# A two-layer attention and mixture-of-experts kernel: the shared expert in one sequence with the destination table in parts, and the returned rows added ahead of the last results

## The chip, the cores and the metric

The kernel runs on one core of a Trainium2 chip. A core has five engines with instruction streams of their own: TensorE (PE, with its weight loads as PEld), VectorE (DVE), ScalarE (ACT), GpSimd (POOL) and SyncE (SP, which here issues transfers); 16 DMA engines carry the transfers of all of them. The metric is the device time of one execution in microseconds (us), the median of three runs.

## What is computed

`x` holds 16 sequences of 112 tokens, 256 wide, all in fp32. Cut to what matters:

```python
# layer zero: cross attention to ctx (16, 375, 256), then 8 experts, best one of 8, F = 704
x = x + tanh(g_xattn[0]) * xattn0(layernorm(x), ctx, mask)
x = x + tanh(g_ffn[0])   * ffn0(layernorm(x))
# layer one: another cross attention, then 8 experts, best two of 8, F = 512
x = x + tanh(g_xattn[1]) * xattn1(layernorm(x), ctx)
x = x + tanh(g_ffn[1])   * ffn1(layernorm(x))

def ffn0(x):                       # ffn1 alike, with two experts a token and softmax weights
    scores = x @ router            # (tokens, 8)
    gate = sigmoid(best score), else 0
    routed = sum over e of (silu(gate_e * x @ w1[e]) * (gate_e * x @ w3[e])) @ w2[e]
    shared = (silu(x @ ws1) * (x @ ws3)) @ ws2
    return shared + routed
```

Each token passes through the shared expert and through one (layer zero) or two (layer one) of eight routed experts.

## The kernel before

Each layer is a chain of stages: setup, attention, shared expert, routed experts. Each engine has a program of its own, written out by hand; semaphores join them, and an engine carries out its instructions in the order in which they are written.

**Attention** is a software-pipelined loop over the sequences; `body(i)` does a different step for several sequences at a time. In its last iterations `first_chunk(l, i - 15)` already makes the first products of the shared expert for the first group.

**Shared expert.** The 16 sequences are taken in groups of four (GT = 4, 448 columns). Of one group, the hidden width F is taken in chunks of 128 rows: six in layer zero (the last one half as high, with gate and up in one matmul, `both`, L1067), four in layer one. A chunk is two matmuls for gate and two for up (`group`, L1138); ACT makes the silu, POOL or DVE the product (POOL at L1782), and `back(g, c)` (L1108) is four matmuls, one for each sequence, that add the chunk's share of the result into PSUM banks 4 to 7. In the order below a matmul call stands once; fp32 calls show as two instructions in the trace, so a chunk has 8 instructions and a back 8. After a group's last back, DVE adds the four results to the residual `x_stream` (`results`, L1451). Layer zero runs four groups ahead of the routed experts, layer one three; its fourth runs late, beside the tail.

**Dispatch.** While the shared expert runs, DVE works out which token goes to which slot of which expert tile (`dispatch`, L1469 to L1600): selection by score (to L1498), on PE the ranks of the tokens (`ranks`, L1075 and L1076, behind the third back of group zero), then a long chain to a one-hot matrix and a table. `table` (L1083) multiplies one by the other on PE, 16 calls in layer zero and 32 in layer one, after the whole of group 1, into one PSUM bank. DVE's `slots` (L1611 to L1624) turn the sums into slot numbers, POOL gathers the tokens' rows with them (L1814).

**Routed experts.** 21 tiles of 128 slots in layer zero, 35 in layer one. For each tile PE turns the gathered rows (`turn`, L1173), multiplies by gate and up weights (L1189), transposes the product (L1212), multiplies by the down weights (L1204); POOL scatters the result to `returned` in HBM (L1823). PE waits ahead of the first tile until DVE has read all results of the last early group: turn, transposes and the results use the same PSUM banks (4 to 7).

**Tail.** After layer one's last tile SP loads the returned rows, 224 KB for each sequence (two rows a token), into a ring of four (L613), and DVE adds them to `x_stream`, two steps for each sequence (L1715, then L1718 that waits for the first), in a loop over the first twelve. PE runs the late fourth group beside it; then DVE adds its four results and the last four sequences' rows. SP stores each sequence (L617) when it is done.

What PE does between group 1 and the end of the early groups is set by these lines of `shared`:

```python
                    for g in range(1, l.early):
                        group(g)
                        if g == 1:
                            table(l)
```

## Time and profile before

| | us |
|---|---|
| median of three runs | 901.02 (899.88 to 901.75) |
| profiled execution, its own time | 905.39 |
| its span in the profile | 903.5 |
| PE busy | 849.7 (94%) |
| DVE, ACT, POOL busy | 376.5, 292.5, 176.4 |
| mean granted clock of PE | 0.97 |

The 16 DMA engines moved 79.12 MB. The span is the time between the first and the last recorded event; the profiled execution's own time lies 1.9 us above it.

How to read the rows further down. In the busy time by stretch a row is: stretch (from:to, us from the span's start), its length, then for PE, PEld, DVE, ACT and POOL the busy time with the count of instructions in brackets, then the granted clock of PE (1.00 is 2.4 GHz, 0.50 is 1.2 GHz), the DMA engines' busy share and GB/s; if it is of one line, only the engines that run this line are given. In the chain of waits a row is start, us, and what the chain went through; "PE ps L1108 x24" is 24 instructions of PE on line 1108 that write PSUM. In the timeline a row is start, duration, engine, line, operation, output<-inputs, count, and in square brackets how long the engine idled just before and what ended it. `x_stream`, `work`, `fixed`, `expert_weights` and the like are areas of memory, `ps` is PSUM; several tensors share one area.

### The profile page before, as it was taken

What the parts mean: (1) busy time and instruction counts of PE and PEld (TensorE: products, weight loads), DVE (VectorE), ACT (ScalarE), POOL (GpSimd) and SP (SyncE); (2) the same over time, 40 slices, a digit from 0 to 9 for tenths busy, and PEclk for the clock granted to TensorE, in tenths of its full rate; (3) what the DMA queues carried; (4) which work ended last, traced back from release to release, by engine and by line L of the source; (5) the groups of instructions that cost most, each with busy time, mean ns of one, the idle gap of its engine ahead of it and who ended that gap; (6) DMA issues with size and microseconds to landing.
All of it is one profiled execution on the core that took longest, in us unless ns stands there. A gap on an engine that the chain in (4) does not pass through costs nothing.

```text
span 903.5 us, 12816 instructions
## 1 busy us (share of the span) xinstructions
PE 849.7 (94%) x3892; PEld 601.9 (67%) x3892; DVE 376.5 (42%) x1361; ACT 292.5 (32%) x693; POOL 176.4 (20%) x202
## 2 busy tenths in 40 slices
PE   6999999999989999999959999999989999999995
PEld 5787786666656766776647888765746666666653
DVE  3689988441211222222246666558111111111117
ACT  2577774320112222122115455531012222222220
POOL 4011101121001222122020100012103333333321
PEclk9999999997998999999979999989799999999998
DMA  7266569003000011012055474400001111111126
GB/s 209 70 195 185 170 204 340 12 0 120 1 34 19 24 36 35 25 36 81 12 144 195 155 240 136 144 21 1 24 6 47 43 45 47 43 47 47 42 62 205
DMA packets 49707, 79.12 MB, mean 88 GB/s; under 512 B 6279, under 2 KB 32397, under 8 KB 49645
## 3 DMA queue, kind: packets, MB, share of 16 engines
q1 hardware_dynamic: 25936, 37.91, 13.9%
q10 hardware_dynamic: 17804, 24.91, 8.3%
q0 software_dynamic: 5904, 15.50, 5.8%
q8 instruction: 36, 0.59, 0.3%
q14 instruction: 27, 0.21, 0.1%
HBM read 65.43 MB, written 12.87 MB: 87 GB/s over the span
## 4 chain that ended last, share of the span: by engine, by line
PE 74%; DVE 3%; issue 2%; ACT 1%; DMA 1%; POOL 0%; SPq 0%; DVEq 0%; ACTq 0%; POOLq 0%
PE ps L1189 25%; PE ps L1204 13%; PE ps L1138 8%; PE ps L1108 7%; PE ps L1212 4%; PE ps L941 2%; PE ps L993 2%; PE ps L1020 2%; PE ps L1083 2%; PE ps L1026 2%; PE ps L1173 1%; PE ps L1059 1%; PE ps L984 1%; DMA work<-returned 1%; PE ps L971 1%
## 5 line engine op out<-in xcount | busy, mean ns | idle before, releaser
L1189 PE MATMUL ps<-expert_weights,work 128*128 x616 | 233.5, 528 | 0.8 <-issue 0.7
L1189 PEld LDWEIGHTS ps<-expert_weights,work 128*128 128x128 f32 x616 | 114.6, 193 | 85.5 <-issue 55.0
L1204 PE MATMUL ps<-expert_weights,work 128*128 x532 | 128.2, 383 | 1.6 <-ACT work L844 1.6
L1204 PEld LDWEIGHTS ps<-expert_weights,work 128*128 128x128 f32 x532 | 99.1, 190 | 39.3 <-issue 25.3
L1823 POOL DMA_INDIRECT returned<-work,ints x56 | 55.4, 989 | 281.2 <-PE ps L1173 228.8
L844 ACT COPY work<-ps 128x512 f32<-128x512 f32 x56 | 32.8, 586 | 212.0 <-PE ps L1212 212.0
L1683 DVE TENSOR_TENSOR work<-work,ps 128x512 f32<-128x512 f32 x35 | 24.1, 688 | 134.8 <-PE ps L1189 134.8
L1770 POOL TENSOR_TENSOR x_stream<-x_stream,layer_constants 112x256 f32<-112x256 f32 x32 | 25.0, 781 | 187.7 <-DVE expert_weights L1362 175.2
L1680 DVE SCALAR_TENSOR_TENSOR work<-ps,work 128x352 f32<-128x352 f32 x42 | 24.5, 584 | 88.4 <-ACT work L837 66.9
L1814 POOL DMA_INDIRECT work<-xn_rows,ints x41 | 40.0, 975 | 105.9 <-PE ps L1173 72.6
L1668 DVE COPY work<-ps 128x256 f32<-128x256 f32 x56 | 23.8, 425 | 82.1 <-PE ps L1204 82.1
L1138 PE MATMUL ps<-xn_turned,work 128*128 128x448 f32 x120 | 49.6, 562 | 0.0
L1108 PE MATMUL ps<-work 128*112 128x256 f32 (+1 forms) x192 | 45.1, 381 | 1.8 <-ACT fixed L748 1.1
L1108 PEld LDWEIGHTS ps<-work 128*112 128x112 f32 (+1 forms) x192 | 33.4, 176 | 15.0 <-issue 6.8
L1138 PE MATMUL ps<-xn_turned,expert_weights 128*128 128x448 f32 x96 | 40.5, 573 | 0.9 <-DVE work L1668 0.9
L1212 PE MATMUL ps<-fixed,work 128*128 128x128 f32 (+1 forms) x266 | 39.4, 277 | 1.6 <-DVE work L1683 0.8
L1026 PE MATMUL ps<-expert_weights,layer_constants 128*128 128x112 f32 x256 | 37.8, 295 | 1.5 <-ACT expert_weights L681 1.5
L1212 PEld LDWEIGHTS ps<-fixed,work 128*128 128x128 f32 (+1 forms) x266 | 30.2, 138 | 13.0 <-issue 6.6
L1026 PEld LDWEIGHTS ps<-expert_weights,layer_constants 128*128 128x128 f32 x256 | 35.6, 209 | 3.8 <-issue 1.8
L837 ACT ACTIVATE work<-ps 128x512 f32<-128x512 f32 x35 | 20.9, 597 | 50.3 <-PE ps L1189 50.3
L1138 PEld LDWEIGHTS ps<-xn_turned,work 128*128 128x128 f32 x120 | 23.5, 198 | 20.4 <-issue 19.8
L1108 PE MATMUL ps<-expert_weights 128*112 128x256 f32 x128 | 32.6, 405 | 2.8 <-POOL expert_weights L1782 2.5
(299 smaller groups left out, 1294.0 us busy)
## 6 DMA issues: line engine op xcount, KB each, us to landing
expert_weights<-in_L_ffn_W_dram ACTq DMA_DIRECT2D x24, 512.0 KB, 4.8
work<-in_ctx_dram SPq DMA_DIRECT2D x32, 336.0 KB
expert_weights<-in_L_ffn_w_eDF_dram ACTq DMA_DIRECT2D x8, 704.0 KB, 5.0
expert_weights<-in_L_ffn_w_eDF_dram SPq DMA_DIRECT2D x8, 704.0 KB, 8.8
xn_rows<-expert_weights ACTq DMA_DIRECT2D x32, 112.0 KB, 2.9
work<-returned SPq DMA_DIRECT2D x16, 224.0 KB, 3.3
expert_weights<-mask_rows SPq DMA_DIRECT2D x16, 164.1 KB, 3.6
expert_weights<-in_L_ffn_w_eFD_dram ACTq DMA_DIRECT2D x4, 640.0 KB, 6.9
```

The costliest lines, as they stand in the source:

```text
L844: nc.scalar.copy(m.midT[:, 0:C1], ps[:, 5, :].rearrange("p (c t) -> p c t", c=C1)).then_inc(m.midT_a.sem, 1)
L1026: ins = mm(ps[:, 3, h * T:(h + 1) * T], w[:, k, h * P:(h + 1) * P], a.tT[:, k], start=(k == 0), stop=(k == KD - 1))
L1108: ins = mm(ps[0:T, 4 + j, 0:D], m.midT_s[0:r, c, j * T:(j + 1) * T], m.ws_back[0:r, c], start=(c == 0), stop=(c == l.FC - 1))
L1138: ins = mm(ps[0:r, up_bank, 0:GN], m.ws_gu[:, half, k, c * P:c * P + r], xnT[:, k, bass.ds(g * GN, GN)], start=(k == 0), stop=(k == KD - 1))
L1189: ins = mm(ps[:, 2 * half + h, 0:l.FH], m.gT[:, u % 2, k], w.rearrange("p a f -> p (a f)"), start=(k == 0), stop=(k == KD - 1))
L1204: ins = mm(ps[:, 7, 0:D], m.midT[0:r, c], w, start=(c == 0), stop=(c == l.FC - 1))
L1212: ins = nc.tensor.transpose(ps[0:r, 5 + c // C1, (c % C1) * P:(c % C1 + 1) * P], m.mid[:, c * P:c * P + r], ident)
L1680: v_.scalar_tensor_tensor(mid, ps[:, 2 + h, 0:l.FH], m.gslot[:, bass.ds(i, 1)], silu, ALU.mult, ALU.mult).then_inc(m.rmid_ready.sem, 1)
L1683: v_.tensor_tensor(mid, silu, ps[:, 2 + h, 0:l.FH], ALU.mult).then_inc(m.rmid_ready.sem, 1)
L1770: g_.tensor_tensor(tile_of(xs, b), tile_of(xs, b), offset[0:T], ALU.add).then_inc(a.xb_ready.sem, 1)
L1814: g_.indirect_dma_start(out=m.g[i % 4], out_offset=None, in_=rows, in_offset=bass.IndirectOffsetOnAxis(ap=slot_token[:, i:i + 1], axis=0)) ...
L1823: g_.indirect_dma_start(out=yg[l.n][:, :], out_offset=bass.IndirectOffsetOnAxis(ap=slot_dest[:, i:i + 1], axis=0), in_=m.yo[:, i % 2], in_ ...
```

## The change

The change has four parts.

1. **The attention's end.** `back(l, 0, 0)` and `back(l, 0, 1)` move into the attention loop's last two iterations (i = 19 and 20). The rest of group zero's backs follow; its last one stands behind group 1's first chunk and the ranks. From there all chunks form one sequence: each chunk is followed by the back of the chunk before it, over the groups' borders too. The ranks write bank 1 instead of bank 2. On DVE, waiting for the iota tables moves behind the selection's first steps; on ACT the gates move behind group 1's first chunk.
2. **The table in parts.** Each part takes 8 calls; there are two in layer zero and four in layer one. They stand between the chunks and backs of group 2, each in a PSUM bank that is free just then (`table_bank`). DVE copies the first part to `m.found` and adds each later part (`found_part`); `slots` works on `m.found` after the last. A chunk that needs a part's bank waits for `tab_read`.
3. **From shared to routed.** `shared` ends with the last early chunk. `routed` does `turn(0)` (in bank 2 for the first two tiles), the last but one back, `turn(1)`, the first tile's gates and ups, the last back, and the first tile's transposes, which wait only for the results that used their bank; DVE reads the results in `read_order` behind the first tile's product.
4. **The tail.** A ring of eight (FR) for the returned rows. DVE adds all 16 sequences' rows in pairs, two first steps and then two second steps, and adds the last group's results after them, each as soon as its back is done (`late_done`). SP stores sequences 12 and 14, ACT 13 and 15. The loops on SP and DVE are written out.

The core of the diff:

```diff
+            def table(l, part):
                 m = B[l.n]
...
+                if part == 0:
+                    pe.wait_ge(m.tab_ready.sem, m.tab_ready.at(1))
+                if part % 2:
+                    pe.wait_ge(m.silu_ready.sem, m.silu_ready.at(n))
+                else:
+                    pe.wait_ge(m.mid_ready.sem, m.mid_ready.at(n))
+                first = part * NB // 2
+                for j in range(first, first + NB // 2):
+                    ins = mm(ps[:, table_bank(part), 0:cols], m.ohc[0:T, j], m.tab[0:T, j], start=(j == first),
+                             stop=(j == first + NB // 2 - 1))
                 ins.then_inc(m.tab_done.sem, 1)
...
+                    if i >= NB + 3:
+                        back(l, 0, i - NB - 3)
...
+            def shared(l):
+                a, m = A[l.n], B[l.n]
+                for c in range(2, l.FC - 1):
+                    back(l, 0, c)
...
+                last = (0, l.FC - 1)
+                for g in range(1, l.early):
                     for c in range(l.FC):
+                        chunk(l, g, c)
+                        if (g, c) == (1, 0):
                             ranks(l)
+                        if (g, c) == (l.early - 1, l.FC - 1):
+                            return
+                        if g == 2 and 0 <= 2 * c - 1 < 2 * l.K:
+                            table(l, 2 * c - 1)
+                        back(l, *last)
+                        if g == 2 and 2 * c < 2 * l.K:
+                            table(l, 2 * c)
+                        last = (g, c)
...
+                    part = 2 * c - 3 if half == 0 else 2 * c - 2
+                    if g == 2 and 0 <= part < 2 * l.K:
+                        pe.wait_ge(m.tab_read.sem, m.tab_read.at(part + 1))
...
+                pe.wait_ge(m.mid_ready.sem, m.mid_ready.at(l.early * l.FC - 1))
                 turn(0, 0)
+                back(l, g, l.FC - 2)
...
+                            if i == 0 and c % C1 == 0:
+                                j = read_order(l).index(1 + c // C1)
+                                pe.wait_ge(m.shared_read.sem, m.shared_read.at(GT * g + 1 + j))
...
+            def found_part(l, part):
...
+                if part == 0:
+                    v_.tensor_copy(m.found, found).then_inc(m.tab_read.sem, 1)
+                else:
+                    dve.wait_ge(m.tab_read.sem, m.tab_read.at(part))
+                    dve.nop(nofuse=True)
+                    v_.tensor_tensor(m.found, m.found, found, ALU.add).then_inc(m.tab_read.sem, 1)
...
-            own.base, own.n = 0, n + GT * l.early
-            shared(l, late=True)
-            dve.wait_ge(m.shared_read.sem, m.shared_read.at(NB))
-            for j in range(GT * l.early, NB):
-                add(j, j % 4)
+            for j in range(0, NB, 2):
+                for b in (j, j + 1):
+                    fin_in = m.fin_in[b % FR]
+                    dve.wait_ge(fin_in.sem, fin_in.at(16 * (b // FR + 1)))
...
+            dve.wait_ge(m.fin_ready.sem, m.fin_ready.at(NB))
+            results(l, NB // GT - 1)
```

Three places show how the instructions move. Line numbers of the kernel after are larger: chunk L1138 is L1158 there, back L1108 is L1127, table L1083 is L1112, turn L1173 is L1212, gates and ups L1189 are L1236, the transposes L1212 are L1266.

On PE in layer one, from the end of group 1 through the table, before:

```order
L1138 MATMUL ps<-xn_turned,expert_weights 128x448 x4
L1108 MATMUL ps<-expert_weights 112x256 x4
L1138 MATMUL ps<-xn_turned,expert_weights 128x448 x4
L1108 MATMUL ps<-expert_weights 112x256 x8
L1083 MATMUL ps<-work 128x35 x32
L1138 MATMUL ps<-xn_turned,expert_weights 128x448 x8
L1108 MATMUL ps<-expert_weights 112x256 x4
```

and after:

```order
L1158 MATMUL ps<-xn_turned,expert_weights 128x448 x4
L1127 MATMUL ps<-expert_weights 112x256 x4
L1112 MATMUL ps<-work 128x35 x8
L1158 MATMUL ps<-xn_turned,expert_weights 128x448 x4
L1112 MATMUL ps<-work 128x35 x8
L1127 MATMUL ps<-expert_weights 112x256 x4
L1112 MATMUL ps<-work 128x35 x8
L1158 MATMUL ps<-xn_turned,expert_weights 128x448 x4
L1112 MATMUL ps<-work 128x35 x8
```

The 32 calls in a row are now four times 8, and chunks or backs of group 2 stand between them.

On PE at layer one's handover, from the last early chunk to the first tile's gates (the rows of the tile's transposes come behind them), before:

```order
L1138 MATMUL ps<-xn_turned,expert_weights 128x448 x4
L1108 MATMUL ps<-expert_weights 112x256 x8
L1173 MATMUL ps<-fixed,work 128x128 x4
L1179 TENSOR_LOAD ints
L1179 ISA x2
L1189 ISA
L1189 MATMUL ps<-expert_weights,work 128x512
```

and after:

```order
L1158 MATMUL ps<-xn_turned,expert_weights 128x448 x4
L1212 MATMUL ps<-fixed,work 128x128 x2
L1127 MATMUL ps<-expert_weights 112x256 x4
L1212 MATMUL ps<-fixed,work 128x128 x2
L1220 TENSOR_LOAD ints
L1220 ISA x2
L1236 ISA
```

and, further on after the gates and ups:

```order
L1236 ISA
L1236 MATMUL ps<-expert_weights,work 128x512
L1127 MATMUL ps<-expert_weights 112x256 x4
L1266 MATMUL ps<-fixed,work 128x128 x4
L1212 MATMUL ps<-fixed,work 128x128 x2
```

The last two backs stood together ahead of both turns; now a back stands between the two turns, and the other one follows the gates and ups.

On DVE in the tail, the end of the program before, with the end of the loop, the late group's results (L1451) and the first of the last four sequences:

```order
L1718 SCALAR_TENSOR_TENSOR x_stream<-work,fixed,x_stream 112x256
L1721 REGISTER_ALU
L1721 COMPARE_AND_BRANCH
L1451 SCALAR_TENSOR_TENSOR x_stream<-ps,fixed,x_stream 112x256 x4
L1715 SCALAR_TENSOR_TENSOR x_stream<-work,fixed,x_stream 112x256
L1718 SCALAR_TENSOR_TENSOR x_stream<-work,fixed,x_stream 112x256
```

and after, where L1792 is the first step and L1797 the second:

```order
L1797 SCALAR_TENSOR_TENSOR x_stream<-work,fixed,x_stream 112x256 x2
L1792 SCALAR_TENSOR_TENSOR x_stream<-work,fixed,x_stream 112x256 x2
L1797 SCALAR_TENSOR_TENSOR x_stream<-work,fixed,x_stream 112x256 x2
L1513 SCALAR_TENSOR_TENSOR x_stream<-ps,fixed,x_stream 112x256 x4
L163 UNCONDITIONAL_BRANCH
```

The results were followed by eight more steps; now they are DVE's last instructions, and the steps come in pairs.

## Rows read from the trace of the kernel before

**Rows 1.** Busy time by stretch: two handovers, routed tiles, tail.

```profile
267.40:280.60 13.20, 9.66 (x29) 5.73 (x29) 2.93 (x7) 1.88 (x5) 0.95 (x1) 0.74 0.22 70
280.60:455.00 174.40, 173.62 (x730) 121.23 (x729) 41.82 (x102) 39.33 (x80) 35.37 (x36) 1.00 0.12 35
...
661.50:672.20 10.70, 7.09 (x18) 3.06 (x18) 2.33 (x5) 1.50 (x4) 0.95 (x1) 0.84 0.04 12
884.00:903.50 19.50, 8.89 (x34) 5.60 (x32) 14.11 (x29) 1.61 (x3) 2.45 (x2) 0.85 0.71 213
```

**Rows 2.** The chain of waits: start, us, what; shared expert and tables.

```profile
184.12 3.01 PE ps L1138 x8
187.12 1.73 PE ps L1108 x8
...
204.24 6.48 PE ps L1083 x32
210.72 8.27 PE ps L1138 x16
...
630.38 9.33 PE ps L1083 x64
639.71 8.82 PE ps L1138 x16
```

**Rows 3.** Busy time by stretch again, of the table's line L1083 alone.

```profile
630.30:634.80 4.50, 4.50 (x42) 4.50 (x42) 1.00 0.00 0
635.00:639.50 4.50, 4.50 (x23) 4.50 (x22) 0.50 0.00 0
```

**Rows 4.** Timeline of PE at the end of the attention, both layers.

```profile
161.82 1.74 PE L1067 MATMUL ps<-xn_turned,work 128*128 128x448 f32 x4 [0.47 <-ACT work L778]
...
164.94 5.43 PE L1108 MATMUL ps<-work 128*112 128x256 f32 x24 [1.08 <-ACT fixed L748]
...
597.67 0.89 PE L1008 MATMUL ps<-fixed,xn_turned 128*112 128x8 f32 x4 [0.88 <-ACT xn_turned L690]
...
598.83 8.03 PE L1108 MATMUL ps<-expert_weights 128*112 128x256 f32 x24 [0.27 <-ACT fixed L748]
```

**Rows 5.** Timeline of PE and DVE within the shared expert.

```profile
202.27 1.98 PE L1108 MATMUL ps<-work 64*112 64x256 f32 x8 [0.72 <-POOL work L1782]
...
604.96 0.29 DVE L1498 TENSOR_TENSOR work<-work 112x128 f32<-112x128 f32 x1
...
607.33 0.29 DVE L1509 COPY work<-ps 112x128 f32<-112x128 f32 x1 [1.44 <-PE ps L1076]
...
627.39 2.13 DVE L1600 TENSOR_TENSOR work<-work 112x1120 f32<-112x1120 f32 x1
...
628.40 1.98 PE L1108 MATMUL ps<-expert_weights 128*112 128x256 f32 x8 [2.17 <-POOL expert_weights L1782]
```

**Rows 6.** Timeline of PE at layer zero's handover.

```profile
269.29 0.41 PE L1173 MATMUL ps<-fixed,work 128*128 128x128 f32 x2 [1.95 <-DVE x_stream L1451]
...
279.55 0.88 PE L1212 MATMUL ps<-fixed,work 128*128 128x128 f32 x6 [0.75 <-DVE work L1680]
```

**Rows 7.** The chain of waits again: a tile's gates and ups.

```profile
289.36 4.74 PE ps L1189 x16
...
664.99 5.41 PE ps L1189 x8
...
678.31 3.44 PE ps L1189 x8
```

**Rows 8.** Timeline of SyncE's queue and DVE in the tail.

```profile
876.41 1.84 SPq L613 DMA_DIRECT2D work<-returned  x4
...
895.78 1.65 DVE L1451 SCALAR_TENSOR_TENSOR x_stream<-ps,fixed,x_stream 112x256 f32<-112x256 f32 x4
...
900.75 0.48 DVE L1718 SCALAR_TENSOR_TENSOR x_stream<-work,fixed,x_stream 112x256 f32<-112x256 f32 x1
```

**Rows 9.** The tail's transfers, 870 to 904 us: queue, packets, MB, share.

```profile
q1 hardware_dynamic: 5888, 5.51, 54.4%
```

More of the change, by code:

```diff
@@ L806, in group @@
                             nc.scalar.copy(m.midT_s[0:r, c], up).then_inc(m.up_copied.sem, 1)
+                        if g == 1 and c == 0:
+                            gates(l)
                 if late:
@@ L860, in _ @@
             shared(l, late=True)
+            m = B[1]
+            for j in range(GT * l.early + 1, NB, 2):
+                act.wait_ge(m.shared_read.sem, m.shared_read.at(j + 1))
+                store(act, j)
         @block.tensor
@@ L1144, in shared @@
-                if not late:
-                    for c in range(l.FC):
-                        back(0, c)
-                        if c == 2:
-                            ranks(l)
-                    for g in range(1, l.early):
-                        group(g)
-                        if g == 1:
-                            table(l)
-                else:
-                    group(NB // GT - 1)
+                if c == 0 and g:
+                    pe.wait_ge(m.shared_read.sem, m.shared_read.at(GT * g))
@@ new lines, in back @@
+                pe.wait_ge(m.mid_ready.sem, m.mid_ready.at(g * l.FC + c + 1))
+                r = l.rows(c)
+                for j in range(GT):
+                    ins = mm(ps[0:T, 4 + j, 0:D], m.midT_s[0:r, c, j * T:(j + 1) * T], m.ws_back[0:r, c],
+                             start=(c == 0), stop=(c == l.FC - 1))
+                    if c == l.FC - 1 and g >= l.early:
+                        ins.then_inc(m.late_done.sem, 1)
+                if c == l.FC - 1 and g < l.early:
+                    ins.then_inc(m.shared_done.sem, 1)
@@ L1222, in _ @@
                 routed(l)
-            shared(LAYERS[1], late=True)
+            shared_late(LAYERS[1])
         @block.vector
@@ L1646, in shared, with middle @@
-                if late:
-                    results(l, NB // GT - 1)
-                    return
-                slots(l)
-                results(l, 1)
-                for g in range(2, l.early):
-                    middles(g)
-                    results(l, g)
+                def middle(g, c):
+                    n = g * l.FC + c
+                    r = l.rows(c)
+                    dve.wait_ge(m.silu_ready.sem, m.silu_ready.at(n + 1))
+                    if (g, c) == (2, 0):
+                        dve.wait_ge(m.shared_done.sem, m.shared_done.at(2))
+                    if not l.half(c):
+                        dve.wait_ge(m.up_done.sem, m.up_done.at(ups(l, g, c)))
+                    up = ps[r:2 * r, c % 2, 0:GN] if l.half(c) else ps[0:r, 2 + c % 2, 0:GN]
+                    v_.tensor_tensor(m.midT_s[0:r, c], m.silu_s[c % 2][0:r], up, ALU.mult
+                                     ).then_inc(m.mid_ready.sem, 1)
@@ L1655, in routed @@
+                for g in range(2, l.early):
+                    for c in range(l.FC):
+                        middle(g, c)
+                        if c == 0:
+                            results(l, g - 1)
+                        for part in (2 * c - 1, 2 * c):
+                            if g == 2 and 0 <= part < 2 * l.K:
+                                found_part(l, part)
+                                if part == 2 * l.K - 1:
+                                    slots(l)
             def routed(l):
```

243 lines of the change are left out of this document (122 added, 121 removed).

## The prediction

> **What bounds the kernel now.** I read the busy time by stretch first. In the routed tiles TensorE (PE) is busy for 173.62 of 174.40 us at the full granted clock [rows 1]: nothing is to be had there without removing work, and the change removes none. So I looked for stretches in which PE idles or runs at the lower of its two clock levels (1.2 instead of 2.4 GHz). The handovers from the shared expert to the routed tiles are such: 9.66 busy of 13.20 at a mean clock of 0.74, and 7.09 of 10.70 at 0.84 [rows 1]. The tail is another kind: PE busy for 8.89 of 19.50, the DMA engines for 71%, VectorE (DVE) for 14.11.
>
> Next I read the chain of waits [rows 2] for what PE's work should cost: 3.01 for a gate and up chunk (8 instructions), 1.73 for a back projection (8). Two chunks behind a table take 8.27 and 8.82, not 6.02. The tables take 6.48 for 32 and 9.33 for 64 instructions. Cut out by itself, the second table [rows 3] shows 42 instructions in 4.50 us at clock 1.00 (0.107 each) and then 23 in 4.50 at 0.50 (0.196): the clock fell inside it, while PE had work without a break. At 0.107 tables of 32 and 64 should cost 3.4 and 6.9.
>
> **Layer zero, part by part.** The attention's end: PE waits 0.47 for ScalarE (ACT) and 1.08 for the last logits [rows 4]. The change puts two back projections (2 x 1.73) where these waits are, and later drops them from the block behind; they need only the chunk products that DVE finished earlier, so the waits are covered: 1.55 saved. The back that waits 0.72 for GpSimd's (POOL's) product [rows 5] now stands behind the next chunk, 3.01 of cover: 0.72 saved. The table: 6.48 - 3.4 = 3.1 if its two parts of 8 calls (16 instructions, 1.7 us each) are at full clock between dense chunks, and the two chunks behind it 8.27 - 6.02 = 2.25. The handover: of the 13.20 [rows 1], 6.85 is work at full clock: three turns of 0.41 and the six transposes 0.88 [rows 6], one tile's gates and ups 4.74 [rows 7]. Now the last two backs lie between the turns and behind the gates and cover the copies and DVE's product. What is left is the transposes' wait for DVE's first result behind the last back, one quarter of 1.65 [rows 8] and two hand-offs, which I take as the 0.75 that these transposes wait for DVE already [rows 6]. Saved: 13.20 - 6.85 - 0.75 = 5.6. Layer zero: 1.55 + 0.72 + 3.1 + 2.25 + 5.6 = 13.2. Bounds: 10.5 if half of the table's and the chunks' gain does not come, 14.0 if the read wait vanishes too.
>
> **Layer one.** At the attention's end two waits of 0.88 (one row stands for both), one of 0.27, and a router step of 0.89 that elsewhere takes 0.47: 2.5 saved. Three backs behind it take 8.03 instead of 3 x 1.73 = 5.19 [rows 4]: 2.84. The 2.17 wait for POOL [rows 5] goes as in layer zero. Table 9.33 - 6.9 = 2.4, chunks 8.82 - 6.02 = 2.8. Handover: 10.70 [rows 1] less three turns 1.23, gates and ups 3.44 [rows 7], four transposes 0.59 (of 0.88 for six) leaves 5.4. Together 18.1.
>
> Here the change adds waits, since PE now comes earlier to DVE's results. The ranks need DVE's selection, whose last steps run at 604.96 [rows 5] and which starts no earlier than before; PE, through the attention's end and one back and one chunk, is there at about 604.5. The wait is about 1.0; chunk (1,1) and all backs are queued behind it. The first table part needs the last step of DVE's chain. That chain takes from 607.33 to 627.39 + 2.13 = 629.52 [rows 5], 22.2 us; from ranks read at 606.1 it ends at 628.3. PE gets from the ranks (605.9) through four chunks and five backs, 20.7, to 626.6. So PE waits between 1.7 and 2.9 (if DVE ends at 629.52 as now); I take 2.2, since DVE's long step shares its stretch with POOL's 3.13 product. Then the read wait of 0.8, as in layer zero. 18.1 - 1.0 - 2.2 - 0.8 = 14.1; bounds 18.1 (none of these waits) and 11.5 (half of the table's and the chunks' gain missing).
>
> What I cost at nothing: copying a table part into the sum has to be done before the next chunk in that bank. DVE's queue holds there one product, four results 1.65 and the copy, 0.29 by the like copy in rows 5; PE's cover is a back of 1.73 and half a chunk, 1.5. That leaves 1.3 for the product. The first gather starts later, behind the last part; its cover is one back and one chunk, 4.74, for the slots' steps, the gather and its landing. Both covers are thin, the second most; if it is gone, the first turn waits, as it does now for 1.95 [rows 6].
>
> A rule on the clock: in rows 3 the clock fell in a run without an idle gap. The Trainium skill, "TensorE: Matmul & The Clock Gate", section "HAM oscillation — how this bites in real kernels", lays such falls to idle gaps between bursts of matmuls; by that the whole saving at tables and chunks would be sure and rival one below impossible. The trace disagrees, so I keep that rival.
>
> **The tail.** Now DVE adds each sequence's two returned rows one behind the other, adds the last group's results at 895.78, then eight more adds, and its last step ends at 901.23 [rows 8], 2.3 before the span's end. After the change all 32 adds come first, in pairs, then four results and the stores. DVE alone would need 16 x 0.82 = 13.1. But the transfers: 5.51 MB use 54.4% of 34 us of all engines [rows 9], 18.5 us for 16 loads (3.67 MB, 0.77 each) and 16 stores (0.39 each). Loads begin at 876.41 [rows 8]; load 15 stands behind 15 loads and about 8 stores: 12.3 + 3.1 from 877.4 on, so it lands near 892.8. The last pair is added by 894.8, results end at 896.5, and the last stores, two queues issuing, at 899.6. Saved: 903.5 - 899.6 = 3.9. Bounds: 2.6 when all twelve early stores go ahead of the last load; 7.0 when all loads go ahead and DVE's adds set the end.
>
> **The sum.** 13.2 + 14.1 + 3.9 = 31.2. The profiled execution took 905.39, so its own time becomes 874.2; the median of the runs, 901.02, lies 4.4 below the profiled one, and becomes 869.8.
>
> **Rivals.** One: the clock falls again, now at a table part or at the handover. Each time costs 5.41 - 3.44 = 2.0 [rows 7] to 2.4 + 2.8 = 5.2. Once in each layer that is 4.0 to 10.4: 873.8 to 880.2, about 876. For it: rows 3, and table instructions, which are short, still stand in a row, though 16 and not 64. Against: each run is shorter than the 42 at full clock in rows 3. Chance 0.13.
>
> Two: the tail is bound by the transfers and gives nothing, since the same 18.5 us of engines [rows 9] lie in the same place. Time: 869.8 + 3.9 = 873.7. For it: DMA share 0.71 in the tail [rows 1]. Against: what now comes after the transfers, the results and eight adds, 1.65 + 3.8, shrinks to the results. Chance 0.08. On the second issuing queue for stores, the Trainium skill, "DMA: Bandwidth & Descriptors", section "Issuing engines are not separate DMA queues", says that transfers issued by several engines share the same 16 engines and only issue time is saved; by it the stores on ACT are worth nothing, as in this rival. No row of before has stores on two queues.
>
> Three: DVE becomes the bound of layer one's shared stage: two more of its steps are held up by POOL's products, 2.17 each as in rows 5, and the gather lands too late, so that the first turn waits 1.95 as now. 869.8 + 4.3 + 1.95 = 876.1. For it: PE is now some 5 us earlier at the same DVE chain of 22.2. Against: four chunks and five backs stand between. Chance 0.11.
>
> Four, the slower side: the clock falls at the first table part and does not come back while parts and chunks alternate, since each part disturbs it anew. The work at full clock from there to the handover is two groups of 5 x 4.74 + 1.74 + 1.73 (the half chunk by rows 4) less one chunk of 3.0, 51.3, and 3.4 of table in layer zero; 16.0 and 6.9 in layer one: 78 us that would double. 869.8 + 78 = 948. It decides when 31.2 of these 78 run at half clock. Against: the two chunks behind a table take 8.27 and not 12.04 [rows 2], so dense chunks bring the clock back while they run. Chance 0.03.
>
> **How the numbers follow.** Forecast 0.65, rivals 0.13, 0.08, 0.11 and 0.03. The likeliest gives 869.8. All lower bounds together (10.5 + 11.5 + 2.6) give 876.4, all upper (14.0 + 18.1 + 7.0) 861.9, which I do not expect at once: 864. At the top 877 takes in rivals two and three and the middle of one. Within 0.2% of before (1.8 us, about what a measurement of this kernel can tell from no change) needs 30 us to be lost, which only part of rival four does: 0.01. Slower is rival four's rest, 0.03; faster 0.96.
>
> **What would show it.** Right: table parts at 1.7 us each and clock 1.00 beside them; chunks at 3.01 behind them; between the last chunk and tile one's gates no idle time over 0.8; waits for DVE of about 1 before the ranks and 2 before the first part in layer one; the last store about 4 us sooner after the first load than now. Wrong: a part at 3 us or a chunk at 4 to 6 (rivals one, four); a turn waiting for a gather, or over 4 us before the first part (three); DVE idle for loads until the end with the span's last 27 us unchanged (two). The prediction fails as a whole if PE's idle time only moves to DVE's chain in both layers.

## The result and the profile after

The changed kernel takes 873.4 us (median of four runs, 872.97 to 874.14) against 901.35 for the kernel before on the same chip: a ratio of 0.969, 95% interval 0.968 to 0.971, 28.0 us faster. The forecast was 869.8 with a range of 864 to 877. The sign and the range hold; the tail, one of the three terms, does not, and part of the 28.0 lies where the change touches nothing.

The span on the page, and busy time by stretch as in [rows 1]: handover of layer zero, handover of layer one, tail.

```profile
span 872.4 us, 12730 instructions
```

```profile
249.60:260.98 11.38, 10.27 (x46) 6.82 (x44) 3.83 (x9) 2.86 (x6) 0.94 (x1) 1.00 0.14 35
...
630.20:640.00 9.80, 8.38 (x36) 5.28 (x35) 2.97 (x6) 1.84 (x4) 2.26 (x3) 1.00 0.16 49
853.00:872.40 19.40, 8.88 (x29) 5.29 (x27) 12.53 (x27) 1.08 (x2) 6.22 (x2) 0.86 0.56 176
```

Both handovers now run at clock 1.00 where [rows 1] had 0.74 and 0.84, and PE is busy for 10.27 of 11.38 and 8.38 of 9.80, with a back projection or two inside. The routed tiles are as before (from 260.98 to 432.00 PE is busy for 170.69 of 171.02, at clock 1.00). The tail still leaves PE idle for half of its time, with the DMA engines less busy (0.56, not 0.71).

The chain of waits at the tables, layer zero first (compare [rows 2]), and layer one's first part and the chunk behind it with their clock:

```profile
198.30 1.91 PE ps L1112 x16
200.21 3.08 PE ps L1158 x8
203.29 1.71 PE ps L1112 x16
```

```profile
608.64 1.97 PE ps L1112 x16
610.62 4.78 PE ps L1158 x8
615.40 1.71 PE ps L1112 x16
```

```profile
608.70:610.60 1.90, 1.90 (x17) 1.90 (x18) 1.90 (x5) 0.00 (x0) 0.00 (x0) 1.00 0.00 0
610.60:615.40 4.80, 4.80 (x12) 2.35 (x11) 0.25 (x2) 0.54 (x1) 0.00 (x0) 0.64 0.00 0
```

A part costs 1.7 to 2.0 at full clock, as forecast, and in layer zero the chunk behind it takes 3.08. In layer one the clock drops behind the first part (mean 0.64 over the next chunk), and that chunk takes 4.78 instead of 3.01: 1.77 lost. It is one fall in each execution, not a chance of this one: the first four kernels of the experiments, which leave this code as it is, show 4.75 to 4.78 at the same chunk.

What PE still waits for in layer one (timeline; idle time before the instruction and what ended it in brackets): ranks, first part, first turn, first transposes.

```profile
585.26 0.47 PE L1097 MATMUL ps<-work,fixed 112*112 112x128 f32 x2 [1.07 <-DVE work L1561]
...
608.64 1.97 PE L1112 MATMUL ps<-work 112*128 112x35 f32 x16 [1.76 <-DVE work L1663]
```

```profile
630.65 0.41 PE L1212 MATMUL ps<-fixed,work 128*128 128x128 f32 x2 [0.45 <-DMA work<-xn_rows,ints]
...
638.84 0.63 PE L1266 MATMUL ps<-fixed,work 128*128 128x128 f32 x4 [0.67 <-DVE x_stream L1513]
```

And the tail: POOL's last product, PE's last back, DVE's last result, and the closing instructions of the program (engine, operation, count; duration in ns as minimum, median and maximum; start in us).

```profile
857.63 5.19 POOL L1853 TENSOR_TENSOR expert_weights<-expert_weights 128x448 f32<-128x448 f32 x1 [3.60 <-ACT expert_weights L818]
...
862.87 3.24 PE L1127 MATMUL ps<-expert_weights 128*112 128x256 f32 x8 [4.23 <-POOL expert_weights L1853]
...
866.15 0.48 DVE L1513 SCALAR_TENSOR_TENSOR x_stream<-ps,fixed,x_stream 112x256 f32<-112x256 f32 x1 [0.37 <-PE ps L1127]
```

```profile
L163 POOLq EVENT_SEMAPHORE  x2: 17/17/17, 872.2 to 872.3; - x2
L163 POOLq DRAIN  x1: 14540/14540/14540, 857.6 to 857.6; - x1
...
L163 SPq DRAIN  x1: 7/7/7, 868.7 to 868.7; - x1
```

SyncE has seen the last store land at 868.7, but the program ends only when POOL's closing drain does, at 857.6 + 14.54 = 872.2. POOL's last product took 5.19, and PE waited 4.23 for it. The kernel before shows 1.32:

```profile
889.90 1.32 POOL L1782 TENSOR_TENSOR expert_weights<-expert_weights 128x448 f32<-128x448 f32 x1 [3.60 <-ACT expert_weights L806]
```

**Where the time went, by stretch.** The times are starts of PE instructions, so that each stretch holds the same work in all kernels: layer zero from its chunk (0,3) to tile one's gates, layer one likewise, and the tail from the last tile's gates to the end of the span.

| | start of chunk (0,3) | layer zero | layer one | tail | POOL's last product |
|---|---|---|---|---|---|
| before | 152.92 | 127.64 | 80.99 | 39.41 | 1.32 |
| changed | 147.53 | 113.45 | 68.73 | 40.55 | 5.19 |
| gain | 5.39 | 14.19 | 12.26 | -1.14 | |
| forecast | 0 | 13.2 | 14.1 | 3.9 | |

The stretches between these are the same within 0.4. The first column is code that no part of the change touches. The row of before is the profiled execution that the forecast used.

### The profile page after: what moved, and what is told of

It is laid out like the page before. It is cut to its first block, busy times and chain, and to the rows that moved or that the text cites. A ratio compares the mean times of both kernels' runs of the same rounds, so it can differ in the third digit from the quotient of the medians.

```text
span 872.4 us, 12730 instructions
## 1 busy us (share of the span) xinstructions
PE 828.9 (95%) x3892; PEld 587.8 (67%) x3892; DVE 377.0 (43%) x1367; ACT 293.1 (34%) x693; POOL 178.4 (20%) x202
## 4 chain that ended last, share of the span: by engine, by line
PE 75%; DVE 5%; issue 2%; ACT 1%; POOLq 1%; DMA 0%; DVEq 0%; ACTq 0%
PE ps L1236 25%; PE ps L1255 14%; PE ps L1158 8%; PE ps L1127 7%; PE ps L1266 4%; PE ps L961 2%; PE ps L1081 2%; PE ps L1013 2%; PE ps L1042 2%; PE ps L1048 2%; PE ps L1212 1%; PE ps L1004 1%; PE ps L1112 1%; PE ps L991 1%; PE ps L1089 1%
## 5 line engine op out<-in xcount | busy, mean ns | idle before, releaser
L1236 PE MATMUL ps<-expert_weights,work 128*128 x616 | 229.1, 520 | 0.8 <-issue 0.8
L1236 PEld LDWEIGHTS ps<-expert_weights,work 128*128 128x128 f32 x616 | 112.7, 190 | 82.7 <-issue 51.4
L1255 PE MATMUL ps<-expert_weights,work 128*128 x532 | 128.2, 383 | 1.6 <-ACT work L860 1.6
L1255 PEld LDWEIGHTS ps<-expert_weights,work 128*128 128x128 f32 x532 | 99.1, 190 | 39.3 <-issue 25.3
L1158 PE MATMUL ps<-xn_turned,work 128*128 128x448 f32 x120 | 47.8, 541 | 0.0
L1127 PE MATMUL ps<-work 128*112 128x256 f32 (+1 forms) x192 | 45.6, 381 | 0.0
L1127 PEld LDWEIGHTS ps<-work 128*112 128x112 f32 (+1 forms) x192 | 33.2, 176 | 12.8 <-issue 6.4
L1266 PE MATMUL ps<-fixed,work 128*128 128x128 f32 (+1 forms) x266 | 39.4, 277 | 1.3 <-DVE x_stream L1513 1.3
L1158 PE MATMUL ps<-xn_turned,expert_weights 128*128 128x448 f32 x96 | 39.8, 561 | 0.8 <-DVE work L1745 0.8
L1266 PEld LDWEIGHTS ps<-fixed,work 128*128 128x128 f32 (+1 forms) x266 | 30.2, 138 | 12.2 <-issue 8.7
L1127 PE MATMUL ps<-expert_weights 128*112 128x256 f32 x128 | 31.9, 394 | 4.3 <-POOL expert_weights L1853 4.2
L1158 PEld LDWEIGHTS ps<-xn_turned,work 128*128 128x128 f32 x120 | 22.6, 190 | 18.2 <-issue 17.4
```

The costliest lines, as they stand in the source:

```text
L1127: ins = mm(ps[0:T, 4 + j, 0:D], m.midT_s[0:r, c, j * T:(j + 1) * T], m.ws_back[0:r, c], start=(c == 0), stop=(c == l.FC - 1))
L1158: ins = mm(ps[0:r, bank, 0:GN], m.ws_gu[:, half, k, c * P:c * P + r], xnT[:, k, bass.ds(g * GN, GN)], start=(k == 0), stop=(k == KD - 1))
L1236: ins = mm(ps[:, 2 * half + h, 0:l.FH], m.gT[:, u % 2, k], w.rearrange("p a f -> p (a f)"), start=(k == 0), stop=(k == KD - 1))
L1255: ins = mm(ps[:, 7, 0:D], m.midT[0:r, c], w, start=(c == 0), stop=(c == l.FC - 1))
L1266: ins = nc.tensor.transpose(ps[0:r, 5 + c // C1, (c % C1) * P:(c % C1 + 1) * P], m.mid[:, c * P:c * P + r], ident)
```

## The experiments

Theory A, formed on this trace: the tail's gain is eaten by POOL. DVE's adds, now in pairs without a gap, keep POOL's last product from running; PE's last back waits for it; and POOL's closing drain, which comes a fixed time behind POOL's last instruction, ends last. Theory B: the transfers bound the tail (the forecast's rival two). Theory C: PE's half clock in the late group does. For the other two terms the question was whether each part is worth what the sum gave it.

Each kernel was timed beside the kernel before on one chip, but not all on the same one. The differences to the changed kernel below are between medians; taken from the ratios to before instead, they come out up to about 2 us otherwise. So a difference of 1 to 2 us says little, and the prices of single parts are read from the stretches, each from one profiled execution.

**The last product on DVE.** POOL makes one product less, DVE makes it between two pairs of adds:

```diff
-            for c in range(LAYERS[1].FC):
+            for c in range(LAYERS[1].FC - 1):
                 middle(LAYERS[1], NB // GT - 1, c, 2 * LAYERS[1].FC)
...
+                if j == 10:
+                    c, n = l.FC - 1, NB // GT * l.FC - 1
...
+                    v_.tensor_tensor(m.midT_s[:, c], m.silu_s[c % 2], m.midT_s[:, c], ALU.mult
+                                     ).then_inc(m.mid_ready.sem, 1)
```

> The changed kernel, except that the last product of the late group (layer one, group 3, chunk 3) is made by DVE, between the adds of sequences 11 and 12, and no longer by POOL. Theory A, POOL: in the changed kernel this product takes 5.19 us on POOL beside DVE's unbroken adds, and POOL's closing drain ends 9.3 us behind it and sets the end of the span. Without it POOL's last product is chunk 2's near 853, its drain ends near 863.4 and is not last; DVE's last result comes near 866.3 and the last store about 2 us later: 3.5 to 4.5 us less than the changed kernel, about 869.3. Theory B, the transfers bound the tail: no change, 873 to 874. Theory C, PE's half clock in the late group bounds it: no change.

Measured: 869.08 (867.21 to 869.54, five runs), ratio to before 0.964, interval 0.962 to 0.966; 4.3 below the changed kernel. POOL's last product, its drain and the last store, timeline and closing instructions:

```profile
852.84 1.13 POOL L1860 TENSOR_TENSOR expert_weights<-expert_weights 128x448 f32<-128x448 f32 x1 [3.50 <-ACT expert_weights L818]
```

```profile
L163 POOLq DRAIN  x1: 10480/10480/10480, 852.8 to 852.8; - x1
...
L163 SPq DRAIN  x1: 7/7/7, 867.3 to 867.3; - x1
```

The drain ends at 852.8 + 10.48 = 863.3 and is no longer last; the store that lands at 867.3 is. Tail 35.71: 3.7 less than before, near the 3.9 that the forecast had. B falls as the cause of the changed kernel's end: SP issues the last load at 857.56 here and at 857.69 there, and yet the span is 867.5 and not 872.4. C falls by the changed kernel's own clock, which was full in the late group until PE had to wait for POOL (busy time of PE alone, then clock, DMA share and GB/s):

```profile
841.00:862.80 21.80, 17.45 (x56) 1.00 0.78 238
862.90:866.20 3.30, 3.21 (x8) 0.58 0.21 59
```

**A small POOL step at the end.** The same kernel, and behind all adds one zero written by POOL into a buffer that is no longer read:

```diff
+            pool.wait_ge(B[1].fin_ready.sem, B[1].fin_ready.at(NB))
+            g_.memset(B[1].fin[0:1, 0, 0, 0:1], 0.0)
```

> The kernel with the last late product on DVE (869.08), and one more thing: when all adds are done, POOL writes one zero into a buffer that nobody reads any more, and ends. Nobody waits for it. Theory A, POOL's closing drain takes 9.3 us from its last step: the adds are done near 863.5, so the span ends near 873 and the time is about 874.5, 5.5 slower. Rival, the drain of 14.5 in the changed kernel was only the starved product, or belongs to its size: no change, 867.5 to 869.5.

Measured: 874.14 (one run).

```profile
862.74 0.09 POOL L1921 MEMSET work<- 1x1 f32 x1 [9.59 <-DVE x_stream L1797]
```

```profile
L163 POOLq DRAIN  x1: 9412/9412/9412, 862.7 to 862.7; - x1
...
L163 SPq DRAIN  x1: 7/7/7, 866.7 to 866.7; - x1
```

A step of 0.09 us that nobody waits for puts the drain's end at 862.74 + 9.41 = 872.2, 5.5 behind the last store (866.7). The drain ends 9.3 us behind POOL's last instruction, be that a product of 1.13 us or this zero.

**Adds unpaired.** The order and the ring stay; each sequence's second step again waits for its first:

```diff
-            for j in range(0, NB, 2):
-                for b in (j, j + 1):
+            for j in range(NB):
+                for b in (j,):
```

> The changed kernel, except that DVE adds each sequence's two rows one behind the other again, with the gap between the two dependent steps; the order (all adds ahead of the last results) and the ring of eight stay. Theory A: POOL's last product takes 1.1 to 1.4 us again, not 5.2, PE's last back starts near 859, POOL's drain still ends 9.3 us behind the product, near 868.3; DVE's adds now last longer (1.2 to 1.37 a sequence, to about 867 to 869), so the whole time is within 3 us of the changed kernel. Theory B: DVE's adds wait for loads, so unpairing costs under 1 us and POOL's product is long as before if it is held by transfers.

Measured: 871.82 (one run).

```profile
857.88 1.31 POOL L1853 TENSOR_TENSOR expert_weights<-expert_weights 128x448 f32<-128x448 f32 x1 [3.50 <-ACT expert_weights L818]
...
859.25 1.98 PE L1127 MATMUL ps<-expert_weights 128*112 128x256 f32 x8 [0.35 <-POOL expert_weights L1853]
```

```profile
L163 POOLq DRAIN  x1: 10663/10663/10663, 857.9 to 857.9; - x1
```

With the gaps POOL's product takes 1.31 and PE waits 0.35; the drain ends at 868.5. DVE's own adds, and the stores behind them, now end the tail (37.99). One run alone would not show that the pairs starve POOL, since the product's length varies; all the profiles together do. With pairs the last product took 1.33, 1.46, 2.61, 5.19 and 6.37 in the five kernels in which POOL makes it; with adds one behind the other it took 1.13, 1.13, 1.25, 1.31 and 1.32 (the kernel before three times, this one and the next). So the pairs can starve it, but do not every time.

**The old tail behind the new rest.** The SP and DVE code of the tail as before, ring of four, loops, stores on SP alone (the diff is the tail part of the change, reversed).

> The changed kernel with the tail of the kernel before: ring of four, one sequence at a time, last group's results ahead of the last four sequences, stores on SP alone, loops kept. The forecast's tail term says that the new tail is worth 3.9: this would be 3.9 slower than the changed kernel, 877.3. Theory A says that the new tail lost what it gained: from the last tile's last copy to the end of the span 30.85 us before against 31.99 now, so this is about 1.1 faster, 872.3.

Measured: 874.36 (873.93 to 875.33, five runs), ratio to before 0.970, interval 0.968 to 0.973. That is 1.0 above the changed kernel by the medians, within the runs' spread; the tail by the traces is 40.49 against 40.55. Neither number fits: not 3.9 slower, not 1.1 faster. With POOL's product starved, the new tail is worth nothing that these runs can tell from zero.

**The backs out of the attention loop.**

```diff
-                    if i >= NB + 3:
-                        back(l, 0, i - NB - 3)
...
-                for c in range(2, l.FC - 1):
+                for c in range(l.FC - 1):
                     back(l, 0, c)
```

> The changed kernel without the two back projections in the attention loop: all backs of group zero but the last stand in one block behind it again; everything else as changed. By the forecast's terms this gives back 1.55 in layer zero and 2.5 + 2.84 in layer one, 6.9 together. But the changed kernel's trace has 1.07 of PE's time ahead of the ranks and 1.76 ahead of the first table part in layer one, waiting for DVE; a later PE uses these up first, so theory A says 1.55 + 5.34 - 2.83, about 4 slower than the changed kernel, and only 2.3 if with these waits the fall of the clock at 610.9 (1.77) goes too.

Measured: 876.72 (875.57 to 881.88, four runs), ratio to before 0.975, interval 0.970 to 0.980: 3.3 above the changed kernel. The stretches: layer zero 116.66 (+3.21), layer one 71.55 (+2.82), tail 38.01 (-2.54, since POOL's last product took 2.61 here). PE's wait in layer one's attention is back, and in layer zero the clock now falls behind the first table part:

```profile
579.07 0.53 PE L1028 MATMUL ps<-fixed,xn_turned 128*112 128x8 f32 x4 [0.88 <-ACT xn_turned L702]
```

```profile
199.59 2.23 PE ps L1110 x16
201.82 4.45 PE ps L1156 x8
```

Of the 3.21 in layer zero 1.52 lies between the starts of chunk (0,3) and of group 1's first chunk, near the term's 1.55, but made up otherwise: two waits of 0.47 for ACT are back, the one of 1.08 is not. The rest is the clock (a chunk at 4.45, a part at 2.23).

In layer one the expectation went wrong in its reason. The wait of 1.07 ahead of the ranks is gone, but the 1.76 ahead of the first part stands as it was: PE and DVE both go on from the ranks, and from their start to the first part it is 23.4 in both kernels (585.26 to 608.64 there, 589.46 to 612.87 here), so a later PE does not shorten the wait. And the fall of the clock behind it is deeper:

```profile
612.87 2.59 PE ps L1110 x16
615.46 5.84 PE ps L1156 x8
```

Some 1.7 of the 2.82 are this fall (1.97 and 4.78 in the changed kernel); only about 1.1 is the attention's end. The three backs there ran at full speed (5.41, against 8.03 in [rows 4]), so this edit does not bring back the term's 2.84.

**The table in one run.**

```diff
-                for j in range(first, first + NB // 2):
+                for j in range(first, first + NB * l.K):
...
-                        if g == 2 and 0 <= 2 * c - 1 < 2 * l.K:
-                            table(l, 2 * c - 1)
                         back(l, *last)
-                        if g == 2 and 2 * c < 2 * l.K:
-                            table(l, 2 * c)
+                        if g == 2 and c == 0:
+                            table(l, 0)
```

> The changed kernel with the table in one run again: 16 calls in layer zero, 32 in layer one, one behind the other at the place of the first part, into one bank, copied once by DVE; the other parts changed as they are. By the forecast the table in a row at falling clock and the chunks behind it cost 3.1 + 2.25 in layer zero and 2.4 + 2.8 in layer one, less 1.77 that the changed kernel still loses: 8.8 slower than the changed kernel. Rival: the clock fell because PE came out of a stretch with idle time, and the dense sequence of chunks alone keeps it up; then under 2 slower, or a little faster, as the gathers come earlier.

Measured: 878.1 (877.55 to 880.2, four runs), ratio to before 0.976, interval 0.972 to 0.980: 4.7 above the changed kernel. The chain in both layers, and the clock in the second table:

```profile
198.98 5.05 PE ps L1112 x32
204.03 5.06 PE ps L1158 x8
```

```profile
612.26 12.24 PE ps L1112 x64
624.50 4.75 PE ps L1158 x8
```

```profile
612.30:614.00 1.70, 1.70 (x16) 1.70 (x16) 1.70 (x5) 0.00 (x0) 0.00 (x0) 1.00 0.00 0
614.60:619.60 5.00, 5.00 (x25) 5.00 (x25) 0.00 (x0) 0.00 (x0) 0.00 (x0) 0.50 0.00 0
```

Layer zero 116.78 (+3.33; the terms said 5.35), layer one 73.02 (+4.29; the terms said 2.4 + 2.8 - 1.77 = 3.4), 7.6 together of 8.8, so the rival (under 2) falls. The whole rises by only 4.7 because the tail is 36.67 here: POOL's last product happened to take 1.33.

**The handover undone.** Both last backs, then DVE's results, then the turns:

```diff
-                turn(0, 0)
                 back(l, g, l.FC - 2)
+                back(l, g, l.FC - 1)
+                pe.wait_ge(m.shared_read.sem, m.shared_read.at(GT * l.early))
+                turn(0, 0)
...
-                    if i == 0:
-                        results(l, l.early - 1)
...
+                results(l, l.early - 1)
                 run_tiles(dve, l, body, 0)
```

> The changed kernel with the handover of before: both last backs, then DVE's four results, then the turns, gates and ups and transposes of the first tile, in both layers; the rest as changed. By the forecast's terms 5.6 in layer zero and 5.4 - 0.8 in layer one come back: 10.2 slower than the changed kernel. Of that about 4 is clock (gates and ups at 7.5 and 5.4 instead of 4.8 and 3.4) and the rest idle time. Rival, that the earlier rows (gathers and slots are ready long before) had already taken most of it: under 5.

Measured: 882.79 (880.88 to 887.1, four runs), ratio to before 0.980, interval 0.976 to 0.983: 9.4 above the changed kernel.

```profile
255.42 0.69 PE L1212 MATMUL ps<-fixed,work 128*128 128x128 f32 x2 [1.75 <-DVE x_stream L1513]
...
257.75 7.15 PE L1236 MATMUL ps<-expert_weights,work 128*128 x16 [0.43 <-ACT work L837]
```

Layer zero 118.87 (+5.42; the term 5.6), layer one 71.52 (+2.79; the term 5.4 - 0.8 = 4.6), tail 41.77 (+1.22, product 6.37). PE's wait for the results is back, and so are gates and ups that run in part at half clock (7.15, against 4.74 at full). The profiled run is the slowest of the four, 887.1; 3.3 of it lie between the two layers' stretches, in layer one's setup and attention, which the edit leaves alone. Layer one is smaller because here its first table part, behind the same wait of 1.76, was not followed by a fall of the clock:

```profile
617.65 1.97 PE ps L1112 x16
619.62 3.09 PE ps L1158 x8
```

Without that, 2.79 + 1.77 = 4.56, the term.

**Layer one's parts one place later.** The first part behind chunk (2,1), where DVE's chain has ended, in the banks that fit the places:

```diff
-                if part == 0:
+                if part == l.n:
                     pe.wait_ge(m.tab_ready.sem, m.tab_ready.at(1))
...
-                first = part * NB // 2
+                first = (part - l.n) * NB // 2
...
-                        if g == 2 and 2 * c < 2 * l.K:
+                        if g == 2 and 0 <= 2 * c - l.n < 2 * l.K:
                             table(l, 2 * c)
```

> The changed kernel with layer one's four table parts each one place later: the first behind chunk (2,1), the last behind back (2,1). Theory A: PE's wait of 1.76 ahead of the first part goes, since DVE's chain ends at 608.58 and PE reaches the new place near 610, and the fall of the clock behind it (chunk (2,1) at 4.78 instead of 3.01) goes with the wait; the last part is now 1.73 nearer to the turn, so the turn's wait for the gather grows from 0.45 to about 2.2. Layer one's stretch from chunk (0,3) to tile one's gates: 68.73 - 1.76 - 1.77 + 1.75, about 67.0. Rival: the clock falls behind the first part also without a wait, since 16 short instructions are what brings it down; then 68.7. The whole time is no measure here, since the tail's length changes with POOL's last product (1.3 to 6.4 us in the runs so far).

Measured: 869.66 (866.08 to 871.63, four runs), ratio to before 0.968, interval 0.964 to 0.971. Layer one's stretch 66.77 (67.0 expected).

```profile
626.35 0.41 PE L1212 MATMUL ps<-fixed,work 128*128 128x128 f32 x2 [2.20 <-DMA work<-xn_rows,ints]
```

```profile
607.30:609.20 1.90, 1.90 (x18) 1.81 (x17) 1.58 (x4) 0.00 (x0) 0.00 (x0) 1.00 0.00 0
...
612.60:615.70 3.10, 3.10 (x11) 1.61 (x11) 0.19 (x1) 0.54 (x1) 0.00 (x0) 1.00 0.03 5
```

Wait and fall are gone, the turn waits 2.20 for its gather, as computed. The profiled run is the fastest of the four; POOL's last product took 1.46 in it, and the tail is 36.75.

**Both, the fastest kernel.** The product on DVE, the parts one place later, and in layer one the last but one back ahead of the first turn.

> The last late product on DVE, as in the kernel that took 869.08, and layer one's table parts one place later; the last but one back of layer one stands ahead of the first turn, as cover for the gather. Theory A: layer one's stretch as in the kernel with the parts moved, about 67.0, less the turn's wait of 2.2, plus 0.4 of the copy that the back no longer hides: 65.2 to 66; the whole 869.1 - 3 = about 866. Rival: DVE's later slots make the gather late by more than the back covers: 868 to 869.

Measured: 866.48 (865.43 to 866.76, five runs), ratio to before 0.963, interval 0.960 to 0.966: 6.9 below the changed kernel. Layer one 66.43, tail 35.25.

```profile
628.75 0.44 PE L1212 MATMUL ps<-fixed,work 128*128 128x128 f32 x2 [0.32 <-DMA work<-xn_rows,ints]
629.74 0.41 PE L1212 MATMUL ps<-fixed,work 128*128 128x128 f32 x2 [0.55 <-ACT work L837]
630.65 3.70 PE L1236 MATMUL ps<-expert_weights,work 128*128 x8 [0.50 <-ACT work L837]
```

The gather is covered (0.32 left), but copies of the turned rows now show (0.55 and 0.50 of waits for ACT): 0.3 better than the parts alone, not the 1 to 1.8 expected.

**The kernel before, twice more.** Its start was of interest, and its table turned out to be.

> The kernel before, profiled once more. Its first profile begins its attention late: the first load lands at 7.16 against 5.75 us and TensorE's clock rises near 43.5 against 34, 5.4 us together ahead of anything that the change touches, and its own time 905.39 lies 4.0 above the median. If that is chance of one execution, this profile shows another start; if it belongs to the kernel before, the same start, and the change is worth these 5 us at a place that it does not touch.

> The kernel before, profiled a third time, for its start alone. So far its chunk (0,3) of layer zero began at 152.92 and at 145.94, and nine profiles of kernels with the changed code began it between 146.7 and 148.2, with the same instructions ahead of it. If the start is chance, this lies anywhere between 145 and 153; from chunk (0,3) on the stretches are 126 to 127.6 (layer zero), 80.8 to 81 (layer one) and 39.4 to 39.9 (from the last gates to the end), as in the first two.

Measured: 897.21 and 897.53. Chunk (0,3) began at 145.94 and 145.96; layer zero's stretch 125.99 and 126.13, layer one's 80.82 and 80.99, the tail 39.93 and 40.00. PE's first instruction in the first profile and in the second:

```profile
7.16 0.35 PE L873 MATMUL ps<-fixed,xn_turned 6*128 6x6 f32 x2 [7.16 <-DMA xn_turned<-in_L_xattn_ln_a_g_dram]
```

```profile
5.96 0.35 PE L873 MATMUL ps<-fixed,xn_turned 6*128 6x6 f32 x2 [5.96 <-DMA xn_turned<-in_L_xattn_ln_a_g_dram]
```

The late start of the first profile (152.92) is of that execution. In the ten profiles of the changed kernel and its variants, with the same instructions up to there, it lies between 145.5 and 148.2. The 29 timed runs of the kernel before spread from 895.8 to 903.7, the four of the changed kernel from 873.0 to 874.1.

The table of layer zero, 6.48 in [rows 2], in the second profile and in the third:

```profile
197.26 5.13 PE ps L1083 x32
```

```profile
197.28 4.66 PE ps L1083 x32
```

The two chunks behind it took 7.98 and 8.47. Table and chunks together are 14.75, 13.11 and 13.13 in the three executions of one and the same kernel.

## Why the prediction was right, and where it was wrong

**The level.** The sum was made against one execution of before, 905.39, whose start was 7 us later than in two others. Against these two the touched stretches gained 12.5 to 12.7 in layer zero, 12.1 to 12.3 in layer one and -0.6 in the tail, some 24; against the first profile 25.3. The medians differ by 28.0. The remaining 3 to 4 are not in the touched stretches. In the one late profile of before most of the excess lies in the start; where it lies in the runs near the median was not measured, and whether the changed program starts better for a reason or by chance is not settled. For the forecast it is luck: with the touched stretches' 24 alone the time would be about 877, the top of the range.

**Layer zero, 13.2 forecast, 12.5 to 14.2 measured: right in sum, with two terms off in opposite ways.** Cut at the same PE instructions, the second profile of before (stretch 125.99) against the changed kernel (113.45) gives 2.76 for the attention's end, 0.80 for the wait for POOL, 3.33 for the table with its chunks and 5.65 for the handover. The terms were 1.55, 0.72, 5.35 and 5.6. The attention's end was worth more because PE had two waits of 0.47 there and the sum counted one, and because short steps beside the waits went too. The table was worth less because the term took one execution's moment for the price: the clock fell within the first 0.6 us of the table in the forecast's profile and 2 to 2.5 us into it in the two others. The undone kernels agree: the table in one run gave 3.33 (5.05 for the table, the clock falling 2 us into it), the handover 5.42; the read wait was 0.67 for 0.75. That the two errors cancel is luck.

**Layer one, 14.1 forecast, 12.3 measured: right but for two prices.** The new waits were priced well: ranks 1.07 (1.0), first part 1.76 (2.2), read 0.67 (0.8). Missing were rival one, which happened once (1.77), and the thin cover of the gather (0.45). With both the sum gives 14.1 + 0.5 - 1.77 - 0.45 = 12.4. The attention's end, cut at the same instructions, is 5.35 against the second profile of before, as the terms' 2.5 + 2.84 had it, though undoing the two backs alone brings back less than half of it; the rest must come with other parts of the change, or is chance of the clock, which no run separates.

**The tail, 3.9 forecast, -1.1 measured: wrong.** The step that failed is the one that took the last store as the end, after costing the transfers, DVE and the stores. These costs were sound: with the last product on DVE the last store is in 23.2 behind the first load's issue (844.10 to 867.3), and the forecast had 23.2 (876.41 to 899.6). But the chain through POOL was not in the sum at all, neither as a release of PE's last back nor as an end of the program. The profile of before had both: [rows 5] show PE waiting 2.17 for a product of POOL's that ran beside a long DVE step, and the closing instructions show POOL's drain:

```profile
L152 POOLq DRAIN  x1: 10668/10668/10668, 889.9 to 889.9; - x1
```

889.9 + 10.67 = 900.6, only 2.9 ahead of the end. A tail shortened by 3.9 had to meet it. The runs give the size: in all kernels whose POOL makes the last product and whose adds are paired, the tail is 35.4 plus that product (35.4 + 5.19 = 40.6 measured 40.55; + 2.61, 38.01; + 1.33, 36.67; + 6.37, 41.77; + 1.46, 36.75). Even a product of 1.13 would leave 36.5, 2.9 less than before and not 3.9. The product's length is a matter of how it meets DVE's adds; what decides that was not found. DVE's adds take both inputs from SBUF, as POOL's product does. The Trainium skill, "SBUF — State Buffer", section "Who interferes with whom", says that a DVE instruction with two SBUF inputs contends with a GpSimd instruction that reads SBUF, and that the port pair they share is an exclusive lock. The traces fit that (1.31 beside adds with gaps, 5.19 beside adds without) and show more: POOL can lose to several adds in a row, not only to one.

**The rivals.** One came true in part, in layer one alone, at 1.77, below the 2.0 to 5.2 given for a fall. Two predicted 873.7 and the time is 873.4, but not by its mechanism: with the same transfers the tail fell to 35.71. Three appeared as 0.45 at the turn. Four did not appear.

## What to carry to other kernels

Before a tail is shortened, list for every engine when it is really through, its closing drain included, and not only the last store: what ended 3 us ahead of the end before can be the end after. When gaps are closed on one engine, look at what ran in them on other engines: here POOL's product had lived on those gaps. And where a sum rests on one profiled execution that lies 4 us off the median, a second profile of the same kernel tells which part of it is chance, also in its terms: here one table cost 4.66 to 6.48.

## What the runs showed of the hardware

- POOL's closing drain ends 9.3 to 9.4 us behind POOL's last instruction in every kernel, be that a product of 1.13 us, one of 6.37 or a zero of 0.09 us.
- POOL's product of 448 columns takes 1.12 to 1.13 at its shortest and up to 6.37 beside DVE's adds without gaps.
- In one and the same kernel the clock fell at different places of an unbroken table of 32 instructions, which took 6.48, 5.13 and 4.66 in three executions.
- The clock's fall behind a table part doesn't follow from the wait ahead of it: with the same 1.76 wait and the same 16 instructions it fell in the changed kernel and in four others with the same code there (the chunk behind at 4.75 to 4.78), more deeply with the backs moved out (5.84), and not with the handover undone (3.09); and with no wait it fell in layer zero with the backs moved out. What decides it stays open; without the wait and with the parts later it did not fall in either kernel.
